# G's products with stationary weight blocks, its rows copied straight into four strips, and zero products at the start

## The reference, cut to what matters

```python
# ids: 16 sequences of 1024 tokens; wte: 1025x64; w1: (16*64)x64; w2: 64x1024; W: 1024x1024
x = [wte[ids shifted by j] for j in 0..15], side by side      # 16*64 numbers for each token
h = tanh(x @ w1 + b1) @ w2 + b2                               # 16 x 1024 x 1024
h = h + autocorrelation_attention(layernorm(h))               # delays of the best correlations
n = layernorm(h)
h = h + n @ W.T + bias + sum_e w_e * ((n @ A_e.T) @ Bf_e.T)   # w = coeffs*scales, 16 experts of rank 16
```

## Time and profile before

| what | value |
|---|---|
| median of 3 runs | 400.08 us (399.44 to 402.02) |
| profiled execution, its own time | 399.41 us |
| its span, first to last instruction | 397.5 us |
| PE matmul busy | 380.2 us (96%), 1908 matmuls |
| PE weight load busy | 276.5 us (70%) |
| DVE / ACT / POOL busy | 276.3 / 246.3 / 214.7 us |
| chain that ended last | PE 84%, POOL 6%, issue 4%, DVE 2%, DMA 2% |

### The profile page before, as it was taken

The page is one execution under the profiler, slowest core; times in us unless marked ns, Lnnn a source line. Parts: engine busy times, 40 slices in busy tenths (PEclk is TensorE's granted clock), DMA queues, the critical chain, the costliest instruction groups (busy, mean ns, idle before and its releaser), DMA issues.

```text
span 397.5 us, 6799 instructions
## 1 busy us (share of the span) xinstructions
PE 380.2 (96%) x1908; PEld 276.5 (70%) x1908; DVE 276.3 (70%) x602; ACT 246.3 (62%) x362; POOL 214.7 (54%) x284
## 2 busy tenths in 40 slices
PE   1998999999999999999999999999999999999993
PEld 1554567777778777777777777777777777777662
DVE  2855567686868777786868687777868696876752
ACT  2524465766667666757666676667576666765642
POOL 6745748475574748374665747473846654312200
PEclk9999999999999999999999999999999999999998
DMA  9793045545545555555455455555554654445475
GB/s 213 216 353 112 12 130 213 187 192 206 209 174 211 192 221 224 211 202 207 172 212 223 157 208 205 221 224 202 200 215 166 223 213 155 203 195 240 194 307 215
DMA packets 28692, 79.86 MB, mean 201 GB/s; under 512 B 7194, under 2 KB 8490, under 8 KB 28676
## 3 DMA queue, kind: packets, MB, share of 16 engines
q1 hardware_dynamic: 23968, 75.19, 48.2%
q0 software_dynamic: 4096, 4.20, 5.3%
q10 hardware_dynamic: 612, 0.27, 0.4%
HBM read 12.40 MB, written 67.12 MB: 200 GB/s over the span
## 4 chain that ended last, share of the span: by engine, by line
PE 84%; POOL 6%; issue 4%; DVE 2%; DMA 2%; SPq 0%; POOLq 0%; DVEq 0%
PE o_ps L1099 46%; PE conv_ps L1190 13%; PE o_ps L1125 7%; PE conv_ps L1196 7%; POOL gathered L405 5%; PE sum_ps L1164 2%; PE sum_ps L1176 2%; PE mix_ps L1176 2%; PE sum_ps L1138 2%; PE et_ps L1144 2%; PE et_ps L1154 2%; DMA extra<-extra 1%; DVE obuf L718 1%; DMA ids_sb<-in_ids 1%; POOL inv_std L440 1%
## 5 line engine op out<-in xcount | busy, mean ns | idle before, releaser
L405 POOL DMA_INDIRECT gathered<-in_wte,idx_now x128 | 128.0, 1000 | 44.1 <-issue 34.3
L518 ACT ACTIVATE obuf<-o_ps,mean_sb,a_sb 128x512 f32<-128x512 f32 x128 | 99.7, 779 | 75.4 <-PE o_ps L1125 47.2
L718 DVE TENSOR_SCALAR obuf<-o_ps,a_sb,mean_sb 128x512 f32<-128x512 f32 x128 | 102.4, 809 | 58.5 <-PE o_ps L1099 33.0
L1099 PE MATMUL o_ps<-w_hi,u_hi 128*128 128x512 f32 x256 | 110.3, 431 | 0.0
L1099 PE MATMUL o_ps<-w_hi,u_lo 128*128 128x512 f32 x256 | 101.2, 395 | 0.0
L1099 PE MATMUL o_ps<-w_lo,u_hi 128*128 128x512 f32 x256 | 101.1, 395 | 0.0
L1190 PE MATMUL conv_ps<-et_hl,shift_hi 128*128 128x512 f32 x256 | 65.4, 397 | 0.8 <-DVE hT L797 0.8
L1099 PEld LDWEIGHTS o_ps<-w_hi,u_hi 128*128 128x128 f32 x256 | 48.1, 188 | 21.5 <-issue 12.6
L1190 PEld LDWEIGHTS conv_ps<-et_hl,shift_hi 128*128 128x128 f32 x256 | 48.1, 188 | 13.5 <-DVE hT L797 1.6
L1099 PEld LDWEIGHTS o_ps<-w_lo,u_hi 128*128 128x128 f32 x256 | 48.1, 188 | 11.6
L1099 PEld LDWEIGHTS o_ps<-w_hi,u_lo 128*128 128x128 f32 x256 | 48.3, 189 | 6.7
(11 more groups left out here) (133 smaller groups left out, 440.7 us busy)
## 6 DMA issues: line engine op xcount, KB each, us to landing
out<-obuf SPq DMA_DIRECT2D x127, 512.0 KB, 2.8
h_all<-in_wT SPq DMA_DIRECT2D x4, 1024.0 KB, 6.5
gathered<-in_wte,idx_now POOLq DMA_INDIRECT x128, 2.9
aT_sb<-in_aT SPq DMA_DIRECT2D x1, 1024.0 KB
bfT_sb<-in_bfT SPq DMA_DIRECT2D x1, 1024.0 KB, 12.2
obuf<-in_w SPq DMA_DIRECT2D x2, 256.0 KB, 7.3
lagged<-xbar_twice SPq DMA_DIRECT2D x1, 512.0 KB, 3.7
out<-obuf SPq DMA_DIRECT2D x2, 256.0 KB, 3.0
```

The costliest lines, as they stand in the source:

```text
L405: pool.indirect_dma_start(gathered[p][:, i, :], None, wte, bass.IndirectOffsetOnAxis(ap=idx_now[p][:, i:i + 1].bitcast(U32), axis=0),).the ...
L518: nc.scalar.activation(obuf[:, q, i % 2, 0:512], o_ps[:, 2 * (i % 2), :], ACT.Identity, bias=mean_sb[pc][:, i:i + 1], scale=a_sb[pc][:, i: ...
L718: nc.vector.tensor_scalar(obuf[:, q, i % 2, 512:L], o_ps[:, 2 * (i % 2) + 1, :], a_sb[pc][:, i:i + 1], mean_sb[pc][:, i:i + 1], ALU.mult, ...
L1099: last = mm(o_ps[:, 2 * (i % 2) + n, :], lhsT, rhs[:, 512 * n:512 * (n + 1)], start=(i % 2 == 0 and f == 0), stop=(i % 2 == 1 and f == len ...
```

## The change

```diff
+            pe.wait_ge(blocks_zeroed, 1)
+            for c in range(IDLE_PRODUCTS):                      # 12
+                mm(et_ps[:, 0:P], moments_two[:, 0:P], moments_two[:, 0:P], start=True, stop=True)
             def weight_product(c, halves):
-                for n in halves:
-                    mm(o_ps[0:E + 1, n, :], w2cT[:, c, :], wT_sb[:, c, 512 * n:512 * (n + 1)], ...)
+                for half in halves:
+                    for n in range(KC // 2):
+                        col = P * (KC // 2 * half + n)
+                        mm(gT_bank(half)[:, n, :], wT_sb[:, c, col:col + P], w2cT[:, c, :], ...)
             def low_rank_products():
-                    for n in range(2):
-                        last = mm(o_ps[0:E + 1, n, :], xaT_sb[:, e, :], bfT_sb[:, e, 512 * n:512 * (n + 1)], ...)
+                    for n in range(KC):
+                        last = mm(gT_bank(n // 4)[:, n % 4, :], bfT_sb[:, e, P * n:P * (n + 1)], xaT_sb[:, e, :], ...)
+            def turn_g():
+                pe.wait_ge(gT_kept, 2)
+                pe.wait_ge(mom_kept, 5)
+                for n in range(KC):
+                    last = tr(o_ps[0:E + 1, 2 + n // 4, P * (n % 4):P * (n % 4 + 1)], gT_sb[:, n, :], ident_sb[:, :])
+                last.then_inc(g_turned, 1)
+                def first_pair():
+                    even_tile(0, strips_last=True)
+                    main_products(1, strips_last=True)
+                    pe.wait_ge(rows_in, 16 * (6 + 12))
+                    for k in range(4):
+                        ins = mm(o_ps[:, k, :], xT[u][rows, 0:P], extra[rows, ...], start=False, stop=True)
+                        if k % 2 == 1:
+                            ins.then_inc(o_done, 1)
                     low_rank_products()
                     conv_half(0)
+                    turn_g()
                     transpose_scaled()
                     conv_half(1)
...
 (ACT)           if in_step(1, g, u):
-                    act.wait_ge(row0_in, 16 * 5)
                     act.wait_ge(g_done, 1)
-                    nc.scalar.copy(w_hi[E:P, :], o_ps[0:E, 0:2, :]...)
-                    nc.scalar.copy(g_hi, o_ps[E:E + 1, 0:2, :]...)
+                    for half in range(2):
+                        nc.scalar.copy(gT_sb[:, 4 * half:4 * half + 4, :], gT_bank(half)).then_inc(gT_kept, 1)
                 if front:
                     keep_odd(0)
+                if in_step(1, g, u):
+                    act.wait_ge(row0_in, 16 * 5)
+                    act.wait_ge(g_turned, 1)
+                    nc.scalar.copy(w_hi[E:P, :], o_ps[0:E, 2:4, :]...).then_inc(g_hi_set, 1)
+                    nc.scalar.copy(g_hi, o_ps[E:E + 1, 2:4, :]...).then_inc(g_hi_set, 1)
...
 (DVE)               scale_h()
-                    g_lo_halves()
+                    g_lo_matrix()
                 if front:
                     add_shifts(0)
+                if in_step(1, g, u):
+                    g_lo_row()
...
 (SP)            for c in range(2, KC, 2):
                 load_wT(c)
-            sp.dma_start(bfT_sb[:, :, :], ...).then_inc(bfT_in, 16)
             sp.wait_ge(mom_kept, 5)
             ... xbar_twice ...
+            sp.wait_ge(rows_gathered[1], 16 * NT)
+            sp.dma_start(bfT_sb[:, :, :], ...).then_inc(bfT_in, 16)
...
+            def row_in_strips(n, row):
+                for i in range(4):
+                    sp.dma_start(extra[XW * i + n:XW * i + n + 1, :].bitcast(F32), row.bitcast(F32)).then_inc(rows_in, 16)
             sp.wait_ge(g_hi_set, 2)
-            for n in (2, 4):
-                row_in(n, g_hi)
+            row_in_strips(2, g_hi)
+            row_in_strips(4, g_hi)
             sp.wait_ge(g_lo_set, 2)
-            row_in(3, g_lo)
-            sp.wait_ge(row0_in, 16 * NX)
-            for i in range(1, 4):
-                sp.dma_start(extra[XW * i:XW * i + NX, :].bitcast(F32), extra[0:NX, :].bitcast(F32)).then_inc(rows_in, 16)
+            row_in_strips(3, g_lo)
```

More of the change, by code:

```diff
@@ L46 @@
 TOPK = 6
+IDLE_PRODUCTS = 12
 PAD = J
@@ L195, in y_view, with gT_bank @@
             return (mix_ps, sum_ps)[hh][:, 0:4 * (E + 3)].rearrange("p (j two n) -> p j two n", j=2, two=2)
+        def gT_bank(half):
+            return o_ps[:, half, 0:KC // 2 * (E + 1)].rearrange("p (n e) -> p n e", e=E + 1)
         def in_pairs(rows):
@@ L489, in _ @@
             act.dma_start(pad_col[:, :], wte[VOCAB:VOCAB + 1, :].rearrange("a e -> e a")).then_inc(pad_in, 16)
+            for n, bank in enumerate((sum_ps, mix_ps)):
+                act.wait_ge(w2T_done, n + 1)
+                nc.scalar.copy(w2cT[:, 4 * n:4 * n + 4, :],
+                               bank[:, 0:4 * (E + 1)].rearrange("p (c n) -> p c n", c=4)).then_inc(w2T_kept, 1)
+            act.wait_ge(b1_in, 32)
+            nc.scalar.activation(hbar[0:E, :], b1_col[0:E, 0:1].to_broadcast([E, P]), ACT.Tanh).then_inc(hbar_set, 1)
             act.dma_start(bias_row[:, :], bias).then_inc(bias_in, 16)
@@ L665, in _ @@
             dve.wait_ge(w2_mean, 1)
-            nc.vector.tensor_scalar(w2c[:, :], w2c[:, :], w2mean[:, 0:1], None, ALU.subtract).then_inc(w2_centred, 1)
+            for n in range(2):
+                cols = slice(HALF * n, HALF * (n + 1))
+                nc.vector.tensor_scalar(w2c[:, cols], w2c[:, cols], w2mean[:, 0:1], None, ALU.subtract).then_inc(w2_centred, 1)
             dve.wait_ge(pad_in, 16)
@@ L1029, in weight_product @@
                     pe.wait_ge(wT_in[c // 2], 16)
-                for n in halves:
-                    mm(o_ps[0:E + 1, n, :], w2cT[:, c, :], wT_sb[:, c, 512 * n:512 * (n + 1)], start=(c == 0), stop=False)
+                for half in halves:
+                    for n in range(KC // 2):
+                        col = P * (KC // 2 * half + n)
+                        mm(gT_bank(half)[:, n, :], wT_sb[:, c, col:col + P], w2cT[:, c, :], start=(c == 0 and n == 0), stop=False)
             def xa_product(first, end):
@@ L1073, in low_rank_products @@
                 for e in range(2):
-                    for n in range(2):
-                        last = mm(o_ps[0:E + 1, n, :], xaT_sb[:, e, :], bfT_sb[:, e, 512 * n:512 * (n + 1)], start=False, stop=(e == 1))
+                    for n in range(KC):
+                        last = mm(gT_bank(n // 4)[:, n % 4, :], bfT_sb[:, e, P * n:P * (n + 1)], xaT_sb[:, e, :], start=False, stop=(e == 1 and n % 4 == 3))
                 last.then_inc(g_done, 1)
+            def turn_g():
[4 more added lines that the diff above has]
+                last.then_inc(g_turned, 1)
             def xbar_correlation():
@@ L1099, in main_products, with even_tile @@
                             last = mm(o_ps[:, 2 * (i % 2) + n, :], lhsT, rhs[:, 512 * n:512 * (n + 1)],
-                                      start=(i % 2 == 0 and f == 0), stop=(i % 2 == 1 and f == len(factors) - 1))
+                                      start=(f == 0 and (i % 2 == 0 or strips_last)),
+                                      stop=(f == len(factors) - 1 and i % 2 == 1 and not strips_last))
                     return last
-                def even_tile(q):
+                def even_tile(q, strips_last=False):
                     if q == 0:
@@ L1113, in even_tile @@
                     ge(pe, ov_kept, NT * c + 2 * q - 1)
-                    main_products(2 * q)
+                    main_products(2 * q, strips_last)
+                def first_pair():
[3 more added lines that the diff above has]
+                    for k in range(4):
+                        rows = slice(XW * k, XW * k + NX)
+                        ins = mm(o_ps[:, k, :], xT[u][rows, 0:P], extra[rows, 512 * (k % 2):512 * (k % 2 + 1)], start=False, stop=True)
+                        if k % 2 == 1:
+                            ins.then_inc(o_done, 1)
                 def four_rank_terms(q):
-                    if q == 0 and in_step(2, g, u):
-                        pe.wait_ge(rows_in, 48)
                     ge(pe, oa_kept, NT * c + 2 * q)
@@ L1243, in step @@
                     return
-                if back:
+                if in_step(2, g, u):
+                    first_pair()
+                elif back:
                     even_tile(0)
@@ L1252, in step @@
                     transpose_rows()
-                if back:
+                if back and not in_step(2, g, u):
                     odd_tile(0)
```

42 lines of the change are left out of this document (24 added, 18 removed).

## The result

The changed kernel takes 405.74 us (median of four runs, 404.86 to 407.72) against 399.76 us (399.06 to 402.02). The ratio is 1.0156, with a 95% interval of 1.0127 to 1.0184: slower by 1.6%. The forecast was 402.8 us and no change that a measurement can tell. The time lies inside the range given, and on the side that had 0.28.

What follows compares the result with a forecast made beforehand. PE, busy throughout the steady loop, bounds the kernel, so only its prologue counts. Terms -1.1 + 0.2 + 2.25 + 1.1 + 0.65 = +3.1 on 399.41 give 402.5, stated as 402.8 us because runs' median exceeds the profile; range 398.5 to 406.0.

Steps and rivals of the forecast that it cites:

- the side that had 0.28: Chance given to a measurably slower result, above the 404.1 us mark; within the marks 0.63, faster 0.09.
- G's products: G's matmuls, paced by 128-column fp32 weight loads at 0.109 us each; four times as many, so no gain.
- The convolution and the strips: Step 1: second convolution 1.35 us later, strips 2.45 later in all, after PE idles of 2.3 and 1.9 us.
- Sequence 1's rows: PE's 1.19 us wait for gathered rows at 30.99 should go with bfT issued later; gain 1.1 us (0 to 1.2).
- rival E: A straggler among the gather's packets holds PE as before, so the 1.1 us is not won: 403.9 us; chance 0.11.
- The start: Zeros and w2c halves bring PE's early products forward 2 to 3 us, but `moments` and `aT` hold the next chain; gain 0.
- rival D: Clock falls to 1.2 GHz while PE waits for `moments`, slowing `aT`'s products and neighbours: about 2.5 us more, 405.3; chance 0.09.
- L1072 above 0.3 us a matmul: Sign that the forecast is wrong through the clock: the 256-column products of `aT` running slower than this.
- 4.2 for G and what hangs on it: Loss terms from G's products to step 2's convolution: 0.2 + 2.25 + 1.1 + 0.65 us.
- 1.1 for the gather: Gain in us from PE no longer waiting for sequence 1's gathered rows, as bfT no longer loads beside them.

Runs made afterwards that it cites:

- e2_fill_gap: Changed kernel plus 13 more zero products on PE ahead of the wait for `moments`; 404.56 us, 1.0133 of before.
- e6_fill_all: e2_fill_gap plus ten zero products before step 1's second convolution and nine before the strips; 404.06 us, 1.0114 of before.
- e8_nine_cols: e2_fill_gap with G's products moving 9 columns instead of 65, other rows of G left out; 417.04 us (one run).
- e9_warm_g: Changed kernel with old strips and first pair, and zero products filling the gaps before `moments`, second convolution and strips; 403.98 us, 1.0121 of before.
- e3_late_bft: Kernel before with only bfT's load issued behind the wait for sequence 1's gathered rows; 399.43 us against 399.49, 0.9993.
- e7_warm_old: Kernel before plus zero products at the start and before `moments`, w2c in halves and late bfT; old G and strips; 400.13 us, 1.0011.
- e4_old_g: Changed kernel without the starting zeros and with G's products in their old form, no turning; 400.82 us, 1.0023 of before.
- e10_turn_first: e2_fill_gap with gT turned ahead of the first convolution and ACT's two casts of G moved earlier; 402.44 us, 1.0079 of before.
- e1_no_zeros: Changed kernel without its twelve zero products at the start; 406.81 us, 1.017 of before.
- e5_g_alone: Changed kernel with G's new form but no zeros, early bfT and the old strips (w2c in halves stays); 405.63 us, 1.0155 of before.

## Why the prediction was wrong

The intervals below are differences of starts shown above, in us; those of the forecast follow from its own times (29.9, 49.1, 56.8 and 63.2).

| stretch | before | forecast | after | e2_fill_gap | e6_fill_all |
|---|---|---|---|---|---|
| start of sequence 1's rows | 30.99 | 29.9 | 33.81 | 29.94 | 31.27 |
| from there to the second convolution | 16.75 | 19.2 | 19.52 | 19.53 | 19.52 |
| from there to the strips | 5.22 | 7.7 | 7.70 | 8.20 | 7.98 |
| from there to step 2's convolution | 7.12 | 6.4 | 7.32 | 7.36 | 6.26 |
| step 2's convolution | 60.08 | 63.2 | 68.35 | 65.03 | 65.03 |

*G's products, wrong by a little.* The pace is 0.1106, for 0.109; e8_nine_cols and L1078 show that the load sets it. Over 144 matmuls the difference is 0.2 us.

*The convolution and the strips, right.* Casts behind the turn, 2.31 us before the second convolution (forecast 2.3), twelve rows 0.62 apart (0.63), and a stall of 1.65 (1.9). The two middle stretches came within 0.3 and 0.0 us. What the text put down to the strips, though, belongs to G: e9_warm_g has the old strips and loses as much. With the old G the direct form costs 0.83, with the new one 0.17.

*Sequence 1's rows, the step that failed in the time and not in the trace.* No wait for the gather is left in after, nor in any kernel with the late bfT (rival E's straggler is not seen). But e3_late_bft and e7_warm_old show nothing of it in their medians. One way to lose it the profiles show: the text took `aT` to land at 14.38 "whatever PE did", but its landing took 10.4 to 12.0 us from issue in these kernels, and PE waited for it 0.40 us in e7_warm_old, 0.98 in e6_fill_all and 1.48 in e4_old_g. Whether this is what the medians lose is not shown.

*The start, wrong; this step failed in mechanism.* The text said that nothing comes of the early work, "Gain 0", and kept the fall of the clock for rival D, 0.09 at +2.5 us. The gap that it had seen itself (9.3 to about 12) became 2.90 us, the clock fell in it, and the nine microseconds behind it ran at 1.2 GHz; the text's own sign of this, L1072 above 0.3 us a matmul, came with (19.15 - 15.60)/8 = 0.44. The price in the profile is 33.81 - 29.94 = 3.9 us, by e2_fill_gap. Mis-sized, too: the text counted `aT`'s products and their neighbours, but the stretch reached over the first group of L1072, the pads, sequence 0's transposes and into the second group. By the medians the fall's price is 0.9 to 1.2 us (e2_fill_gap), and their intervals overlap; the profiled run was the longest of four. Nor does taking out the zeros help, which the text did not see: it costed the narrow products by their loads at either clock, and never asked what a train of them does to the clock.

*The second fall, not seen.* Behind the 2.31 and 1.65 us of standing that the text itself had forecast, the clock fell once more, between 62 and 63: the last stretch took 7.32, for 6.26 in e6_fill_all, 1.06 us. Filling both gaps, or making them shorter (0.52 and 0.92 us in e10_turn_first), removed it; which of the two gaps it needs no run here separates.

*The account.* The forecast was +3.1: 4.2 for G and what hangs on it, less 1.1 for the gather. With the clock held up (e6_fill_all) the whole change costs 404.06 - 399.89 = 4.2 us by the medians of that batch, which is the first term alone: the 1.1 is not in the time (in the profile `aT`'s late landing took it). With the clock as it falls, it costs 405.74 - 399.76 = 6.0. The 2.9 us from 402.8 to 405.74 are therefore about 1.1 for a gain that the medians never showed and about 1.8 for the clock. The last number is less sure than the mechanism: the intervals of after (1.0127 to 1.0184), e2_fill_gap (1.0096 to 1.0170) and e6_fill_all (1.0070 to 1.0157) overlap in this order, and of the kernels with G's new form only e10_turn_first (1.0051 to 1.0107) stands apart from after. That the falls are there, and what stands around them, the traces show. Rival D was the case, then, on top of the forecast's own mechanism, as its own sum had it. That its 405.3 lies near 405.74 is partly luck: it still held the 1.1 for the gather and knew of no second fall, and its 2.5 for the first is neither the 3.9 of the profile nor the 0.9 to 1.2 of the medians. With the gap already worked out, 0.09 was too little for it.

## What to carry over

A sum over durations that are right can fail by the clock: for every gap that a change opens or widens before the steady loop, and for every train of narrow matmuls under wide loads, write down what the stretch behind it costs at 1.2 GHz, and treat that as a term and not as a remote rival. Turning a product round so that it needs a transpose back puts a ring PE, ACT, PE, ACT, DVE, DMA at the end of it; look for the slot in which all of the ring lies under other work before doing it. And a wait that goes away in the trace is no gain until the medians of a dozen runs hold it.

## What the runs showed of the hardware that was not expected

The clock is not held up by a busy PE alone. In e1_no_zeros and e5_g_alone PE worked from 7.7 us on with no gap over 0.33 us, on matmuls of 65 columns under loads of 128, and stood at 1.2 GHz through the first group of `aT`'s products (3.62 us, until 18.4 and 18.5). In e8_nine_cols, with 9 columns, it fell after 31 us out of a train without a gap, and PE stayed there over the 48 narrow products that followed. In after and e4_old_g it was low behind waits of 2.90 and 1.48 us; e6_fill_all waited 0.98 us for `aT` and kept it. The Trainium skill (TensorE: Matmul & The Clock Gate, HAM oscillation) tells of waits between bursts that throttle the clock, with which after (a wait for DVE) and e4_old_g (a wait for DMA) agree in kind; it doesn't cover the fall of e8_nine_cols.

Which property of those trains it is, one pair of kernels tells in part. Up to the fall e8_nine_cols differs from e2_fill_gap only in the columns that G's matmuls move, 9 for 65; the loads, the order and nearly the pace (0.106 and 0.111 us) are the same, and the granted clock of e2_fill_gap is 1.00 from 30 to 56 us. So the few columns moved let it fall, as far as one execution of each can show. On the way up it stays open: e4_old_g, where the clock was up at 12.24, differs from e1_no_zeros in loads and columns at once.

The clock's column in the profile reads 1.00 until the first recorded change, though the durations there are those of 1.2 GHz (3.62 us for eight products of 256 columns in e1_no_zeros, under 1.00). For the early microseconds durations are the better witness.
